# Regrouping the query tiles of an index stage, and moving weight preparation out of its loop

## What is computed

```python
iq = (hidden_states @ idx_wq_w).reshape(b, s, IDX_H, IDX_D)
ik = hidden_states @ idx_wk_w
iw = hidden_states @ idx_weights_w * IDX_H ** (-0.5)
idx_scores = jnp.einsum('bqn,bnqk->bqk', iw, jax.nn.relu(jnp.einsum('bqnd,bkd->bnqk', iq, ik))) * IDX_D ** (-0.5)
idx_scores = jnp.where(causal, idx_scores, -jnp.inf)
_, topk_idx = jax.lax.top_k(idx_scores, TOPK)
scores = jnp.where(mask[:, None], scores, -jnp.inf)
return out @ o_w
```

## Time and profile before

| | us |
|---|---|
| median of 3 runs | 1438.15 (1436.08 to 1439.1) |
| the profiled execution, its own time | 1438.22 |
| its span, first to last instruction | 1436.4 |
| PE busy | 1316.1 (92% of the span) |
| DVE busy | 1091.6 (76%) |
| ACT busy | 833.0 (58%) |
| POOL busy | 660.9 (46%) |

### The profile page before, as it was taken

How to read it: one execution, slowest core, us unless ns; L and a number is a source line. 1 busy time by engine, 2 the same in 40 slices (tenths; PEclk the granted TensorE clock), 3 DMA queues, 4 the chain that set the end, 5 groups by cost and what they waited for, 6 DMA issues and landing times.

```text
span 1436.4 us, 21267 instructions
## 1 busy us (share of the span) xinstructions
PE 1316.1 (92%) x7147; PEld 1096.2 (76%) x7147; DVE 1091.6 (76%) x2226; ACT 833.0 (58%) x1819; POOL 660.9 (46%) x651
## 2 busy tenths in 40 slices
PE   2968999999899789998769999999999999999998
PEld 1756888888789677775457888888888888888876
DVE  6357334343647599999979998898989889888976
ACT  3783532233246566774557767666776776667761
POOL 5460210010037445645656556555665565566534
PEclk9978999999999899998679999999999999999999
DMA  6560310000212333654720000000000000000021
GB/s 212 159 186 1 117 37 1 1 20 0 69 39 67 107 91 117 227 177 147 276 93 14 1 29 28 28 29 28 19 10 28 28 29 28 29 28 1 16 81 59
DMA packets 83706, 95.52 MB, mean 67 GB/s; under 512 B 11792, under 2 KB 59280, under 8 KB 83088
## 3 DMA queue, kind: packets, MB, share of 16 engines
q1 hardware_dynamic: 83600, 94.17, 20.9%
HBM read 75.27 MB, written 18.87 MB: 66 GB/s over the span
## 4 chain that ended last, share of the span: by engine, by line
PE 68%; DVE 17%; ACT 5%; issue 3%; DMA 2%; SPq 1%; POOL 1%; ACTq 0%; DVEq 0%
PE ps L350 16%; PE ps L352 15%; PE ps L351 15%; PE ps L1877 9%; PE ps L1897 3%; PE ps L1896 3%; DVE acc L1398 3%; DVE top L1409 2%; DVE xn_l L1471 1%; DVE rop L1421 1%; DVE acc L1412 1%; DVE rop L1419 1%; DVE pm L1451 1%; DMA iwq_raw<-in_L_attn_idx_wq_w 1%; DVE rop L1420 1%
## 5 line engine op out<-in xcount | busy, mean ns | idle before, releaser
L753 POOL TENSOR_SCALAR pm<-pm,smx 128x128 f32<-128x128 f32 (+1 forms) x255 | 189.4, 751 | 207.7 <-DVE smx L1458 207.7
L1055 ACT ACTIVATE pm<-pm,smx 128x128 f32<-128x128 f32 (+7 forms) x256 | 197.3, 772 | 35.3 <-DVE smx L1451 34.4
L1451 DVE CUSTOM_DVE_ANT_0 pm<-ps,mbias 128x128 f32<-128x128 f32 (+7 forms) x256 | 191.5, 752 | 27.4 <-PE ps L1877 13.1
L1877 PE MATMUL ps<-ident,pm 128*128 128x128 f32 x1152 | 175.0, 276 | 7.3 <-DVE pTa_l L1471 2.0
L1061 ACT ACTIVATE xn_h<-ps 128x512 fp32r<-128x512 f32 (+3 forms) x256 | 128.6, 513 | 84.1 <-PE ps L1877 81.3
L1471 DVE TENSOR_TENSOR xn_l<-ps,xn_h 128x512 fp32r<-128x512 f32 (+3 forms) x256 | 144.5, 587 | 24.8 <-ACT xn_h L1061 23.8
L350 PE MATMUL ps<-latT_l,qc_h 128*128 128x512 f32 (+3 forms) x384 | 143.3, 373 | 16.7 <-DVE smx L1451 8.7
L1877 PEld LDWEIGHTS ps<-ident,pm 128*128 128x128 f32 x1152 | 132.3, 141 | 33.9 <-issue 11.3
L352 PE MATMUL ps<-latT_h,qc_h 128*128 128x512 f32 (+3 forms) x384 | 134.1, 349 | 0.0
L351 PE MATMUL ps<-latT_h,qc_l 128*128 128x512 f32 (+3 forms) x384 | 133.6, 348 | 0.0
L1398 DVE SCALAR_TENSOR_TENSOR acc<-ps,iw,acc 128x768 f32<-128x768 f32 (+4 forms) x105 | 87.2, 877 | 25.1 <-ACT ps L941 24.6
(11 more groups left out here) (294 smaller groups left out, 3717.8 us busy)
## 6 DMA issues: line engine op xcount, KB each, us to landing
iwq_raw<-in_L_attn_idx_wq_w SPq DMA_DIRECT2D x48, 256.0 KB, 3.5
base<-in_L_ffn_mean_w SPq DMA_DIRECT2D x28, 256.0 KB, 3.1
wring<-in_L_ffn_w SPq DMA_DIRECT2D x21, 256.0 KB, 3.8
ow_raw<-in_L_attn_o_w SPq DMA_DIRECT2D x8, 512.0 KB, 3.9
xn_t<-in_L_attn_o_w SPq DMA_DIRECT2D x8, 512.0 KB, 4.2
wuvo<-pr_even SPq DMA_DIRECT2D x8, 512.0 KB, 5.1
wuvo<-pr_hl SPq DMA_DIRECT2D x8, 512.0 KB, 4.7
wuvo_h<-wuvo SPq DMA_DIRECT2D x16, 256.0 KB, 2.6
```

The lines of the kernel that those rows point to most:

```text
L753: pool.tensor_scalar(pm[:, i % 4, 0:w], pm[:, i % 4, 0:w], smx[:, 32 + i:33 + i], 0.0, ALU.mult, ALU.add).then_inc(hd_p, 1)
L1055: act.activation(pm[:, i % 4, 0:w], pm[:, i % 4, 0:w], ACT.Exp, bias=smx[:, i:i + 1], scale=-1.0, accum_out=smx[:, 16 + i:17 + i]).then_in ...
L1451: dve.tensor_tensor_reduce(out=pm[:, i % 4, 0:w], in0=two_banks(2 * (i % 2), w), in1=mbias[:, TRI[t]:TRI[t + 1]], scale=1.0, scalar=3.0 * BIG,
L1877: done = pe.transpose(ps[:, t_bank(p, i), tile(k)], pm[:, tq % 4, tile(4 * c + k)], ident[:])
```

## The change

The same work is cut elsewhere. The groups become tiles 1, 2, then 3, 4, then 5, 6, 7, so that the projections are 256, 256 and 384 columns wide. The first group keeps four single banks, the second two bank pairs, the third gets three pairs (2, 3), (4, 5) and (6, 7). Only four head pairs stay in the loop, at steps 20, 23, 26 and 29, all of them in the second group's steps; twelve follow behind it. PE waits for the fourth pair's eviction ahead of score tile 65, the first in banks 6 and 7, and the first pair behind the loop now waits for the last sum. POOL's order and ACT's steps behind the loop are shifted by four pairs; the high half R3 of the last rotation moves from behind the masks to behind pair 11, and pairs 12 to 15 stand at the end. ACT makes three masks instead of two, POOL four instead of five. SP gives `hd_go` ahead of `load_wuvo(0)` rather than behind it.

```diff
-INDEX_TILES = ((1, 2, 3), (4, 5), (6, 7))
-INDEX_COLS = ((P, 512), (512, 768), (768, 1024))
+INDEX_TILES = ((1, 2), (3, 4), (5, 6, 7))
+INDEX_COLS = ((P, 384), (384, 640), (640, 1024))
+INDEX_SUMS = (32, 64, 112)
-PAIR_AT = {24: 0, 28: 1, 32: 2, 34: 3, 37: 4, 39: 5, 42: 6, 44: 7}
+PAIR_AT = {20: 0, 23: 1, 26: 2, 29: 3}
 TAIL_ORDER = [(_step[0], int(_step[1:])) for _step in
-              "P8 F0 F1 P9 F2 F3 P10 P11 M0 P12 L0 M1 P13 L1 M2 P14 L2 P15 M3 L3".split()]
-TAIL_ACT = {8: "F0 F1", 9: "F2 F3", 11: "E0 E1", 12: "R0 E2", 13: "R1 E3", 14: "R2"}
+              "P4 F0 F1 P5 F2 F3 P6 P7 M0 P8 L0 M1 P9 L1 M2 P10 L2 P11 M3 L3 P12 P13 P14 P15".split()]
+TAIL_ACT = {4: "F0 F1", 5: "F2 F3", 7: "E0 E1", 8: "R0 E2", 9: "R1 E3", 10: "R2", 11: "R3"}
...
         def score_bank(n):
-            return 2 + n % 4 if n < 48 else 2 + 2 * (n % 2)
+            return 2 + n % 4 if n < 32 else 2 + 2 * (n % (2 if n < 64 else 3))
...
         def slot_free(n):
-            return n - 3 if n < 48 else max(48, n - 1)
+            return n - 3 if n < 32 else max(32, n - 1) if n < 64 else max(64, n - 2)
...
             store_pair(PAIRS - 1)
-            sp.wait_ge(tk_mask, 5)
-            load_wuvo(0)
             for m in range(2):
                 sp.wait_ge(pr_st[m], 48 * PAIRS // 2)
             sp.wait_ge(en_st, 32)
             sp.drain().then_inc(hd_go, 1)
+            sp.wait_ge(tk_mask, 4)
+            sp.wait_ge(tk_last, 1)
+            load_wuvo(0)
...
-            rotate_hi(0, 3)
...
                     reach(pe, ix_acc, slot_free(n))
+                    if n == 65:
+                        pe.wait_ge(pr_out_w, LATER)
...
-                if j == LATER + 1:
+                if j == LATER:
                     pe.wait_ge(ix_acc, 7 * IDXH)
```

More of the change, by code:

```diff
@@ L638, in drop_later @@
             def drop_later(phase):
-                pool.wait_ge(ix_acc, (48, 80, 112)[phase])
+                pool.wait_ge(ix_acc, INDEX_SUMS[phase])
                 for t in INDEX_TILES[phase]:
@@ L671, in topk_mask @@
                 for k, t in enumerate(INDEX_TILES[phase]):
-                    pool.wait_ge(tk_rep, (45, 78)[phase] + k + 1)
+                    pool.wait_ge(tk_rep, INDEX_SUMS[phase] - 1 + k)
                     pool.tensor_scalar(mbias[:, TRI[t]:TRI[t + 1]], acc_of(t), TAKEN, BIG, ALU.is_gt, ALU.mult)\
@@ L1032, in _ @@
             for k, t in enumerate(INDEX_TILES[2]):
-                act.wait_ge(tk_rep, 110 + k + 1)
+                act.wait_ge(tk_rep, INDEX_SUMS[2] - 2 + k)
                 act.activation(mbias[:, TRI[t]:TRI[t + 1]], acc_of(t), ACT.Relu, bias=shift[:], scale=SHRINK)\
                     .then_inc(tk_last, 1)
-            rotate_hi(0, 3)
             def sum_half(p, i):
@@ L1405, in topk_round @@
                         dve.wait_ge(ix_mask, t + 1)
-                        reach(dve, tk_rep, (0, 48, 80)[step // IDXH])
+                        reach(dve, tk_rep, (0, 32, 64)[step // IDXH])
                     else:
@@ L1429, in _ @@
                 topk_round(step)
-            dve.wait_ge(tk_mask, 5)
+            dve.wait_ge(tk_mask, 4)
             dve.wait_ge(hd_go, 1)
@@ L1447, in head_period @@
                         reach(dve, hd_tr, NG * (p - (i < 4)) + GROUPS[(i - 4) % 16][-1][1] + 1)
-                        if p == 0 and 6 <= i < NT:
-                            dve.wait_ge(tk_last, i - 5)
+                        if p == 0 and 5 <= i < NT:
+                            dve.wait_ge(tk_last, i - 4)
                         dve.wait_ge(hd_s, 16 * p + i + 1)
```

## The result

The changed kernel takes 1463.71 us (median of 4 runs, 1458.27 to 1464.30), the kernel before 1437.14 beside it: ratio 1.0176, interval 1.0163 to 1.0190. Slower was right; the size was not: +26.6 us where +11 stood in the sum, and 1463.7 lies above the upper end of the range, 1458. The profiled execution took 1464.3 us, its span is 1462.5.

A forecast was written before the change was run, and what follows sets the result against it. PE was taken to bound group one, DVE group two and group three's top-k. First head operation +12.2 us, minus 1.0 at the heads' start, made +11 on 1438.22: 1449 us; own range 1445 to 1454, with A and B 1441 to 1458.

The forecast's parts named there:

- The pairs decide the tail: Behind the last sum: twelve pairs' stores end after DVE's top-k, first head operation 12.2 us later, against 6.3 by DVE's path.
- Group three: Steps 32 to 47: DVE and PE level at 5.98 us a step, 89.7 where it was 84.8, a loss of 4.9.
- The hole: Between the last latent piece and the next sum, 11.6 us waiting behind pair 0's load; no edit touches it: 0.
- A: Tail: at full clock pairs land before DVE's longer top-k, which is last; 1444 us, chance 0.22.
- B: Group two: index weights come late, queued on SP behind a pair's load, four times 1.7 us; 1456 us, chance 0.12.
- C: Group two: PE is not the limit, steps run at DVE's pace, 13.2 us less; 1436 us, chance 0.10.
- Steps 0 to 8: Group one: sums shrink to 7.3 us, plus 17.2 unchanged latent work and 1.2 waits, 25.7 from 32.6: gain 6.9.
- The start itself: Before the first sum: two projections of 256 columns instead of 384 stand ahead of it, 1.4 us earlier.
- Steps 9 to 16: Group one: PE's step falls from 4.0 to 2.58 us, 11.4 gained, 0.7 given back for POOL's value copies.
- Group two: Steps 16 to 31: PE sets the pace with four pairs; 66.5 us from the hole's end instead of 74.0, gain 7.5.
- Pair 4's wait for the last sum: Start of the tail: pair 4 waiting for the last sum adds 0.2 us until the eighth pair's products.
- ScalarE being ready: Start of the heads: masks and table load done while pairs finish, up to 2 us back, 1.0 taken.

## Why the prediction was off

**Right: what ends last in each stage.** The pairs decide the tail, by 11 us over the top-k (forecast 6). VectorE's rounds are 6.16 us (first replace at 736.54, the next at 742.70), its tail 101.6. Group three takes 89.25 where 89.7 stood. The hole stayed at 11.7. The last six pair cycles are 8.6, 8.6, 8.0, 10.0, 8.0 and 4.8, each within 0.1 of the sum, R3's among them. Two lines of the chain around R3's cycle, products' end to transposes:

```profile
719.36 0.66 PE L1759 MATMUL ps<-ident,kvb_raw 64*128 64x64 f32 x4 [2.22 <-ACT pr_out L966]
...
729.27 0.66 PE L1759 MATMUL ps<-ident,kvb_raw 64*128 64x64 f32 x4 [4.10 <-ACT pr_out L966]
```

**Rivals.** A fell: `hd_go`, not the top-k, is last, and with the clock raised it still came 7.7 us behind the last replace (1.73 with the index weights first and R3 back too). Its premise that activity would lift the clock is half true: from 690 us on the change's own pairs left it at 0.50, added work lifted it to 0.8, and the cycle moved by little as long as R3 and the rotary evictions stood in it. B fell as a mechanism: ScalarE waited for index weights once in group two, 0.74 us. C fell by 3 us in three steps: with a pair they take 13.50 (rows below; the next three take 13.51). The weight-load busy time that spoke for it came from a stretch in which VectorE set the pace; in the new one PEld is busy 56.8 of 70.7 us, more than VectorE with 52.2, and TensorE sets the pace.

```profile
503.30 1.54 DVE L1399 SCALAR_TENSOR_TENSOR acc<-ps,iw,acc 128x512 f32<-128x512 f32 x2 [2.71 <-ACT ps L943]
...
516.80 1.54 DVE L1399 SCALAR_TENSOR_TENSOR acc<-ps,iw,acc 128x512 f32<-128x512 f32 x2 [2.71 <-ACT ps L943]
```

**The mis-sized terms** (15 us in all, nearly all in one direction). The mechanism held; what failed are sizes, above all those of groups one and two and of pair 4's wait:

1. *Steps 0 to 8*, -6.9 forecast, -2.8 measured. The step that failed is "17.2 of latent work that the edit leaves alone" and "1.2 for waits". The sums did fall as worked out. But VectorE's idle time was 3.6 us where 1.2 had been put (3.5 before: nothing had said that it would fall), and the latent work took some 2 us longer, since with shorter steps more of GpSimd's operations stand beside it. TensorE waited for GpSimd twice, where the kernel before has no such wait behind its first sum:

```profile
425.94 0.39 PE L351 MATMUL ps<-ikT_l,iqT_h 128*128 128x256 f32 x1 [2.06 <-POOL iqT_l L650]
432.31 0.39 PE L351 MATMUL ps<-ikT_l,iqT_h 128*128 128x256 f32 x1 [1.25 <-POOL iqT_l L650]
```

 The start itself came 2.6 earlier, not 1.4, but 1.3 of it is the first layer's (above): the term was right, and luck hid a part of the miss. "Cover: ACT and POOL were busy 46.8 and 46.6 of 67.9 us" compared totals; the operations of a single step are what must fit.
2. *Steps 9 to 16*, -10.7 forecast, -8.4 measured. The step of 2.58 is there (2.57 to 2.63 in most), but two of them took 3.4 and 3.7: GpSimd's value copies cost 1.1 rather than 0.7, and TensorE came out of a wait of 3.50 us for VectorE at the lower clock (256 columns in 0.41 instead of 0.28). These account for some 1.2 of the 2.3; the rest is spread.
3. *Group two*, -7.5 forecast, -3.3 measured. Two steps failed. "Three steps take 12.8 on PE, 13.0 with waits" is 13.50: waits and restarts of 0.7, a freed bank's 0.5 among them, where I had put 0.2, and not even that 0.2 was in the sum: its 51.1 is four times 12.8. Over the twelve steps it was 3.1 more. And "9.6 for three plain steps" behind the hole took 12.6 (484.36 to 496.91), 3.0 more. TensorE, 10.4 us without work, restarts at the lower level, and the run with the index weights first, where it does not, puts 2.3 us on that. Before, VectorE's step of 4.65 had hidden the restart. The end of the stretch gave 1.8 back.

```profile
485.25 0.77 PE L351 MATMUL ps<-ikT_l,iqT_h 128*128 128x512 f32 x1 [10.42 <-DVE acc L1399]
485.81 0.63 PE L352 MATMUL ps<-ikT_h,iqT_l 128*128 128x512 f32 x1
...
491.04 0.40 PE L352 MATMUL ps<-ikT_h,iqT_l 128*128 128x512 f32 x1
```

4. *Pair 4's wait for the last sum*, 0.2 forecast, 4.4 measured (its products end 9.1 us behind the last sum, pair 8's ended 4.7 behind it), and 4.9 at the sixth pair's products, from where the forecast counts cycles. The wait is not the cost, but what stands behind it: the transposes of pair 4, those of the final weights and those of pair 5 now all come after the last sum, and at the lower clock. The run with two bank pairs has 3.7 of it back.

```profile
644.51 0.66 PE L1759 MATMUL ps<-ident,kvb_raw 64*128 64x64 f32 x4 [2.76 <-DVE acc L1399]
```

5. *Small ones.* The last store took 3.22 us instead of 2.19 (+1.0), the drain 0.2 instead of 1.0 (-0.8), and nothing of the 1.0 for ScalarE being ready came back.

Where a stage's new length was the old one less the work that goes, the gain came out too large; where the length was built from measured operations of the engine that sets the pace (group three, the rounds, the last pair cycles), it held. The range was the other fault: 2 us either way for each of groups one and two, where they missed by 5 and 4 us and in the same direction. A shorter step with the same fixed work in it is behind much of both; the restart is a second cause.

Not tried, and in both kernels' tails: TensorE waits for a pair's weights, 4.61 us ahead of 686.09 in the changed kernel and 3.89 ahead of 693.63 before, while the DMA queues move 360 GB/s (675 to 690 us, changed kernel).

## What to carry to other kernels

Before a table of steps is changed, add up the work of the one engine that every stage needs and look where it idles: an order that does not shorten that work can gain from its idle time alone. Here 17.0 us of it lay open in group one and became 14.2, while group two and the tail went from 1.6 to 29.6. A gain from shorter steps is to be checked step by step against the fixed work of the other engines in that very step, not against their busy share of the stretch. And look for the load that stands behind a blocked one in the same queue: three loads moved ahead of a blocked one were worth 10 us, where the new tables cost 27.

## What the hardware showed unasked

- A VectorE operation of 64 columns with two SBUF inputs takes 0.27 us alone and up to 1.31 beside GpSimd; index sums out of PSUM are not touched (607 and 609 ns).
- TensorE's clock was granted at 0.50 (the lower level) from 690 to 735 us, with TensorE busy 10 to 11 of each 15 us, and at 0.8 in the mean, so at the upper level for part of the time, with the added products. Busy time alone does not tell the level: from 675 to 690 us the changed kernel's TensorE was busy 10.4 of 15 at a granted clock of 0.83. Halving the products' time there left the cycle of two pairs at 8.6 us, because ScalarE and GpSimd wait for each other in it.
- The Trainium skill ("TensorE: Matmul & The Clock Gate", What's actually happening) calls the lower level the default that activity lifts; the stretch that rose when work was added agrees; the one that stayed low shows that work as such was not enough there.
